# A two-layer graph network on one core: the gather loop, its tables and the order of the dense stages rewritten

## What is computed

```python
norm = -dinv[src] * dinv[dst]                       # dinv: 1/sqrt(degree)
def conv(x, W0, W1, b):
    tx1 = segment_sum(x[src] * norm[:, None], dst)  # gather rows, add them by target
    return x @ W0 + tx1 @ W1 + b
h = conv(x, W1_0, W1_1, b1)
h = layer_norm(h) * gamma + beta
h = where(h >= 0, h, 0.01 * h)
x = layernorm(x + conv(h, W2_0, W2_1, b2))
```

## Time and profile before

| | |
|---|---|
| runs without the profiler | 2444.04 us (2441.0 to 2445.28) |
| span of the profiled execution | 3370.7 us (the page gives no other time of it) |
| before the first gather | 201 us |
| layer 1, first to last gather | 201 to 1727 us |
| layer 2, first to last gather | 1775 to 3334 us |
| PE, DVE, ACT, POOL busy | 61%, 46%, 15%, 50% of the span |

### The profile page before, as it was taken

How to read it: one execution, slowest core, us unless ns; L and a number is a source line. 1 busy time by engine, 2 the same in 40 slices (tenths; PEclk the granted TensorE clock), 3 DMA queues, 4 the chain that set the end, 5 groups by cost and what they waited for, 6 DMA issues and landing times.

```text
span 3370.7 us, 41016 instructions
## 1 busy us (share of the span) xinstructions
PE 2065.1 (61%) x7250; PEld 963.6 (29%) x7251; DVE 1544.4 (46%) x3507; ACT 505.3 (15%) x1030; POOL 1700.9 (50%) x1725
## 2 busy tenths in 40 slices
PE   6836576665665665665764656565565656555655
PEld 5712232222222322232331222222222222222222
DVE  6754444444444444544443444444444434444444
ACT  5920111111111211111230000000000000000000
POOL 0156554545555554655526545554545445554543
PEclk6558887887887878887876878787777777878778
DMA  6376565655555555655646555565555555555554
GB/s 215 133 259 181 150 174 155 173 159 160 164 167 168 159 165 157 181 159 167 182 132 200 166 158 171 166 177 155 167 159 164 155 158 165 161 165 162 159 159 122
DMA packets 215109, 559.98 MB, mean 166 GB/s; under 512 B 48100, under 2 KB 49760, under 8 KB 214948
## 3 DMA queue, kind: packets, MB, share of 16 engines
q0 software_dynamic: 133120, 436.31, 45.9%
q10 hardware_dynamic: 44676, 81.73, 7.2%
q1 hardware_dynamic: 37152, 40.21, 3.6%
HBM read 493.08 MB, written 64.18 MB: 165 GB/s over the span
## 4 chain that ended last, share of the span: by engine, by line
PE 30%; another core or an unknown queue 26%; issue 25%; DVE 8%; ACT 5%; DVEq 3%; ACTq 1%; DMA 1%; POOL 1%; SPq 0%; POOLq 0%
PE bank L749 16%; PE bank L710 10%; DVE acc L947 6%; PE bank L668 2%; ACT work L556 2%; ACT feat L564 1%; DVEq L923 1%; PE bank L727 1%; PE bank L655 1%; DVEq L947 1%; DVE onehot L923 1%; POOL ring L444 1%; ACT work L546 1%; ACTq L528 0%
## 5 line engine op out<-in xcount | busy, mean ns | idle before, releaser
L444 POOL DMA_INDIRECT ring<-table,index x1664 | 1672.6, 1005 | 1466.5 <-SPq L393 952.1
L947 DVE SCALAR_TENSOR_TENSOR acc<-bank,down,acc 128x512 f32 x928 | 696.9, 751 | 1219.6 <-PE bank L710 709.8
L710 PE MATMUL bank<-ring,onehot 128*128 x3712 | 920.3, 406 | 306.0 <-issue 148.1
L749 PE MATMUL bank<-wA,feat 128*128 128x512 f32 x784 | 547.6, 863 | 804.2 <-ACT feat L564 748.2
L923 DVE TENSOR_SCALAR onehot<-count_h,dst_c,neg_tile 128x128 f16<-128x128 f16 x1856 | 489.2, 329 | 490.1 <-issue 487.6
L710 PEld LDWEIGHTS bank<-ring,onehot 128*128 128x128 f16 x3712 | 380.6, 103 | 865.6 <-issue 515.3
L749 PEld LDWEIGHTS bank<-wA,feat 128*128 128x128 f32 x784 | 212.0, 285 | 1084.9 <-ACT feat L564 774.3
L727 PE MATMUL bank<-wB,base_in 128*128 128x512 f32 x784 | 353.6, 594 | 0.0
L546 ACT ACTIVATE work<-acc 128x512 f32 (+1 forms) x98 | 61.7, 630 | 1747.4 <-issue 1039.3
L727 PEld LDWEIGHTS bank<-wB,base_in 128*128 128x128 f32 x784 | 149.5, 191 | 155.8 <-issue 142.1
L564 ACT ACTIVATE feat<-bank 128x512 f32<-128x512 f32 x98 | 58.5, 597 | 845.4 <-remote 828.7
(11 more groups left out here) (118 smaller groups left out, 689.6 us busy)
## 6 DMA issues: line engine op xcount, KB each, us to landing
ring<-table,index POOLq DMA_INDIRECT x1664
base_in<-feat ACTq DMA_DIRECT2D x98, 256.0 KB
feat<-feat SPq DMA_DIRECT2D x49, 256.0 KB, 2.9
table<-work SPq DMA_DIRECT2D x49, 256.0 KB, 3.1
feat<-feat ACTq DMA_DIRECT2D x49, 256.0 KB
table<-work ACTq DMA_DIRECT2D x49, 256.0 KB
feat<-in_x ACTq DMA_DIRECT2D x48, 256.0 KB
out<-work ACTq DMA_DIRECT2D x48, 256.0 KB
```

The source lines that it names most:

```text
L444: nc.gpsimd.indirect_dma_start(out=ring[:, at * ROW:(at + 1) * ROW], out_offset=None, in_=table[l], in_offset=bass.IndirectOffsetOnAxis(ap ...
L710: last = nc.tensor.matmul(bank[u % SUM_BANKS][:, :], onehot[:, u, j, :], ring[:, bass.ds(at, D)], start=j + half == 0, stop=j + half == GROUP)
L749: last = nc.tensor.matmul(to[:, :], feat[:, 2 + tile_slot, c * P:(c + 1) * P], wA[:, c * D:(c + 1) * D], start=False, stop=c == KB - 1)
L947: nc.vector.scalar_tensor_tensor(tile_of(acc, tile[u]), bank[u % SUM_BANKS][:, :], col(down[:, l, :], tile[u]), tile_of(acc, tile[u]), ALU ...
```

## The change

1. **Gathers.** The `bounds_check` register and `oob_is_err=False` are gone, and the indices are read straight from the columns of one table `index` for all 832 chunks; SP's copies L371 go. POOL's and SP's loops are written out in full.
2. **Register tables.** For each step one row of `step_u` (u16) holds the group and the four ring offsets, ready to be loaded; `tile_u` holds the offset of the tile in `acc`. PE and DVE are written out in full, four steps to a register load.
3. **One-hots.** `rel[:, n*2+j]` (fp16) holds, for each step's chunk, the targets relative to the step's tile. It is made ahead of the loop by 14 comparisons (`pick`) and 14 matmuls on PE. DVE then writes the one-hots of four steps (eight chunks) in one `tensor_tensor` of 128x1024 instead of eight `tensor_scalar` of 128x128.
4. **Adds.** The scale `down` is no longer applied in each step; a tile's sums are turned by a matmul with a scaled identity, `diag`, that ACT writes.
5. **Dense stages.** A visit now turns the sums of tile v and multiplies those of tile v-1 (moved by ACT since the visit before). The later stages lag 2 and 3 visits, not 3 to 6. Layer norm reads PSUM in layer 1. Visits come every 9.47 steps, at any step.
6. **Ahead of the first layer.** DVE makes the steps' tables after the first 8 of the 49 rows of L878 (L876 in the new file), not after all 49. The load of `wA` waits for `picked`.

```diff
@@ SP
-                def pass_on(it, l=l):
...
-                    if it.least + 2 < GATHER_BLOCKS:
-                        stage_index(it.n + 2, it.slot)
+                for g in range(GROUPS):
...
+                    sp.wait_ge(ring_landed[k], 16 * GROUP * ((GROUPS * l + g) // RING + 1))
+                    sp.sem_inc(groups_ready[l], 1)
@@ GpSimd
-            bound = pool.snap(pool.to_reg(N - 1))
...
-                            nc.gpsimd.indirect_dma_start(
-                                out=ring[:, at * ROW:(at + 1) * ROW], out_offset=None, in_=table[l],
-                                in_offset=bass.IndirectOffsetOnAxis(ap=index[:, it.slot, at:at + 1], axis=0),
-                                bounds_check=bound, oob_is_err=False).then_inc(ring_landed[k], 16)
+                        nc.gpsimd.indirect_dma_start(
+                            out=ring[:, at * ROW:(at + 1) * ROW], out_offset=None, in_=table[l],
+                            in_offset=bass.IndirectOffsetOnAxis(ap=index[:, c:c + 1], axis=0)
+                        ).then_inc(ring_landed[k], 16)
@@ VectorE
-                        last = nc.vector.tensor_scalar(onehot[:, slot, j, :], count_h[:, :],
-                                                       col(dst_c, group * GROUP + j), col(neg_tile, n),
-                                                       ALU.subtract, ALU.is_equal)
+                nc.vector.tensor_tensor(onehot[:, b % 2, :, :], count_h[:, :].unsqueeze(1).to_broadcast([P, HOTS, P]),
+                                        rel[:, b * HOTS:(b + 1) * HOTS].unsqueeze(2).to_broadcast([P, HOTS, P]),
+                                        ALU.is_equal).then_inc(onehots_ready, 1)
...
-                        nc.vector.scalar_tensor_tensor(tile_of(acc, tile[u]), bank[u % SUM_BANKS][:, :],
-                                                       col(down[:, l, :], tile[u]), tile_of(acc, tile[u]),
-                                                       ALU.mult, ALU.add).then_inc(sums_added, 1)
+                    nc.vector.tensor_tensor(acc_at, acc_at, bank[n % SUM_BANKS][:, :], ALU.add).then_inc(sums_added, 1)
@@ VectorE, ahead of the first layer
+            for b in range(EDGE_BLOCKS):
+                for j in range(GROUP):
+                    last = nc.vector.tensor_scalar(pick[b][:, :, j], group_f, (j - b * P) / GROUP, part_group[:, 0:1],
+                                                   ALU.add, ALU.is_equal)
@@ TensorE, in a visit
+                    dense(to, base_in[:, k.slot, :], wB, True)
...
+                    pe.wait_ge(sums_moved, TILES * l + k.n + 1)
+                    dense(to, sums_t[k.slot], wA, False).then_inc(out_done, 1)
+                if it.within(0, TILES):
...
+                    for c in range(KB):
+                        last = nc.tensor.matmul(bank[TURN_BANK][:, c * P:(c + 1) * P],
+                                                acc[:, bass.ds(it.n * D + c * P, P)], diag[:, it.slot, :],
+                                                start=True, stop=True)
+                    last.then_inc(sums_turned, 1)
```

More of the change, by code:

```diff
@@ L31 @@
 U32 = mybir.dt.uint32
+U16 = mybir.dt.uint16
 ALU = mybir.AluOpType
@@ new lines, in step @@
+            def step(l, n, entry):
+                g = STEPS * l + n
+                for j in range(GROUP):
+                    hot = onehot[:, n // BLOCK % 2, n % BLOCK * GROUP + j, :]
+                    for half in range(2):
+                        if j + half == 0:
+                            if n % BLOCK == 0:
+                                pe.wait_ge(onehots_ready, g // BLOCK + 1)
+                            if n == 0:
+                                wait(pe, sums_added, g - SUM_BANKS + 1)
+                            pe.wait_ge(groups_ready[l], entry[0])
+                        if j == GROUP - 1 and half == 1 and n + 1 < STEPS:
+                            wait(pe, sums_added, g + 1 - SUM_BANKS + 1)
+                        last = nc.tensor.matmul(bank[n % SUM_BANKS][:, :], hot,
+                                                ring[:, bass.ds(entry[1 + 2 * j + half], D)],
+                                                start=j + half == 0, stop=j + half == GROUP)
+                last.then_inc(steps_done[l], 1)
@@ new lines, in _ @@
+            for l in range(2):
+                for n in range(STEPS):
+                    if n % BLOCK == 0:
+                        entry = nc.values_load_multi_w_load_instructions(
+                            step_u[0:1, n * ENTRY:(n + BLOCK) * ENTRY], engines=[mybir.EngineType.PE], min_val=0,
+                            max_val=RING * GROUP * ROW - D, skip_runtime_bounds_check_because=WALK_FITS)[1]
+                    step(l, n, entry[n % BLOCK * ENTRY:(n % BLOCK + 1) * ENTRY])
+                    for v in range(TILES):
+                        if place(v) == n + 1:
+                            with pe.If(early > v):
+                                visit(numbered(v), n + 1, l)
+                visits_late(pe, early, (LAG_HIDDEN, LAG_SUMS)[l], lambda it, steps: visit(it, steps, l), True)
@@ L861, in _ @@
+            assert all(place(v) == FIRST_PLACE + (v * SPACING >> 8) for v in range(BOUNDS)) and place(BOUNDS) == STEPS
+            link(nc.vector.tensor_scalar(place_i[:, 0:1], part_i[:, :], SPACING, None, ALU.mult))
             link(nc.vector.tensor_scalar(place_i[:, 1:2], place_i[:, 0:1], 8, None, ALU.arith_shift_right))
             link(nc.vector.tensor_copy(place_f[:, 0:1], place_i[:, 1:2]))
-            link(nc.vector.tensor_tensor(place_f[:, 1:2], place_f[:, 0:1], part[:, :], ALU.add))
@@ L873, in _ @@
[L873 to L874 removed]
+            nc.vector.tensor_tensor(late[0:BOUNDS, 1:2], late[0:BOUNDS, 0:1], bound_f[0:BOUNDS, 2:3], ALU.mult
+                                    ).then_inc(walk_cmp, 1)
             def low_rows(it):
@@ L898, in _ @@
+            for b in range(2):
+                hots(0, b)
             dve.wait_ge(s_bias, 32)
```

728 lines of the change are left out of this document (372 added, 356 removed).

## The result

The changed kernel takes 2773.86 us (2768.18 to 2783.63, four runs) against 2444.18 us (2441.0 to 2445.28, four runs): ratio 1.136, 95% interval 1.133 to 1.1385. It is slower by 330 us, and 464 above my 2310. Its profiled execution has a span of 2766.3 us, like its runs.

What follows compares the result with a forecast made beforehand. The prediction took POOL's back-to-back gathers, 1.305 us apart, to bound the kernel. It summed 2444 - 225 (gathers) + 89 (one-hots) + 10 (start) - 9 (layer change) = 2309, said 2310 us; its own range 2230 to 2430, wider 2120 to 2545.

Steps and rivals of the forecast that it cites:

- What bounds the kernel before: POOL's gathers, one after the other: 1664 x 1.305 us plus 286.0 around them, 2457.5 against 2444.0 in runs.
- the 913 us of waits in the profiled execution: Other waits in POOL's gather loop, most traced to ACT's late L564; taken as mostly the profiled execution's own.
- PE needs 17.8 us in a tile: PE's 8.4 us of steps plus 9.4 of visit, against POOL's 22.2: 4.4 us to spare per tile.
- the visits, "only cover": Dense-stage visits: PE's shorter waits free time POOL's bound didn't need; 18.1 us of PE a tile, no gain counted.
- Gathers, 1.305 to 1.17: Removing the bounds check shortens the distance between POOL's gathers: 1664 x 0.135 = 225 us less, range 0 to 391.
- the check costs nothing: Rival: gather distance stays 1.305 us and the one-hots stall gathers by 80 us: 2525, slower; chance 0.34.
- One-hots, +89: DVE's two-input one-hot instruction, taken at 1.13 us, delays gathers starting beside it: 89 us more; 22 at 0.57 us.
- Adds 0: DVE's L947 adds without the scale save nothing, since DVE has 6 us to spare; PE's diag turn is hidden.
- start +10: DVE makes the tables after row 8, 13 us in which ACT stops: 10 us more until the first gather.
- layer change -9: Gap between layers, 48.2 us: the last visits' drain goes from 6 visits to 3, 9 us less.
- the unrolled program starves for instructions (nothing in the trace speaks for it): Rival on instruction supply, dismissed since PE's matmuls follow at 0.22 us with a register instruction between; no chance given.
- The prediction's last sign: POOL's waits for SP should be short; if long although its distance fell, PE or the transfers bind.

Runs made afterwards that it cites:

- p1: Kernel before without the gathers' bounds check, two register tables in 16 bits, undisturbed: 2362.0 us, ratio 0.966.
- h1: Kernel before with the second gather of each group left out from the ring's second turn, two tables in 16 bits, undisturbed: 2044.7 us, ratio 0.836.
- late sets: The three sets of experiments (first, second, fourth) beside which the kernel before took 3442 to 3453 us.
- n2: Changed kernel with PE loading 8 numbers per four steps, not 20, and the gathers' bounds check put back, undisturbed: 2545.0 us, ratio 1.043.
- m1: Changed kernel with PE loading 8 numbers (four 16-bit, four 32-bit) per four steps in place of 20, undisturbed: 2469.6 us, ratio 1.011.
- n1: Changed kernel with PE's 8-number loads and a block's one-hots written by eight tensor_scalar instructions, undisturbed: 2388.4 us, ratio 0.977.
- undisturbed: Condition of the four sets of experiments beside which the kernel before took 2442 to 2445 us.
- e1: Kernel before without the gathers' bounds check, two register tables in 16 bits, kernel before at 3448.7 us: 3443.7 us, ratio 0.9997.
- the first set: Four variants, one of the kernel before and three of the changed kernel, run where the kernel before took 3448.7 us.
- the sixth: Two variants of the changed kernel with small PE loads, scalar one-hots or the check put back, run where the kernel before took 2442.2 us.

## Why the prediction was wrong

**What bounds the kernel before: right.** The gathers did: p1, with shorter gathers and somewhat longer register loads, falls by 83 us where 1664 x (1.305 - 1.25) = 92 were to be had, and h1 falls to PE's side. That the 913 us of waits in the profiled execution weren't part of the runs of 2444 us was right too. Their origin was not: they aren't the profiler's, since the same kernel takes 3440 without it in the late sets. And "PE needs 17.8 us in a tile" was right within 1% (h1: 2044.7 for 2030).

**The step that failed: the visits, "only cover", with 18.1 us of PE a tile after the change.** I counted PE's matmuls and waits and none of the instructions of its sequencer. Part 2 of the change, the register tables, has no line in the prediction at all; under the gathers and the rivals I wrote that register work costs nothing, from rows where it was one instruction between gathers or matmuls. The change makes PE load 40 numbers in eight steps in place of 16, in 16 bits each, and the load of 4.73 us per four steps can't be hidden behind 3.6 us of matmuls, the less as it starts 2.0 us into them. PE's side went from 17.8 to 25 us a tile, above POOL's 21 to 22: +304 us. The numbers in reach before the run were two rows of the trace that I hadn't asked for (L698 above: 0.59 for eight numbers). They would have given 20 x 0.074 = 1.5 us, too little to show, by this estimate; in the traces it is the width of the number that makes 4.7 of it. A changed kernel with 20 numbers of 32 bits was not run.

The Trainium skill has the figure, in "Runtime: NRT & Kernel Launch", "Instruction fetch mechanics": about 200 ns for a register in a `TENSOR_LOAD`, also in bulk (the page speaks of the runtime's own loads, from HBM). For 16-bit numbers this case's traces agree (0.236 us each at 20, 0.238 at 14, 0.25 at 4), for 32-bit ones they don't (0.074 at 8, 0.083 at 4). By it an estimate of the load is 20 x 0.2 = 4.0 us, which is already above the block's 3.6 us of matmuls: it spoke against this change, and I didn't look for it. The floor of some 600 ns that the Trainium skill, in "DMA: Bandwidth & Descriptors", "Latency and other measured facts", gives for such a load isn't seen: four 32-bit numbers take 0.33.

**Gathers, 1.305 to 1.17: mis-sized.** The distance became 1.25 (0.95 + 0.30), worth 92 us and not 225; measured 83 (p1) and 75 (n2 against m1). The check is 0.055 of the 1.00 us, about an eighteenth, where I had guessed an eighth or a little more; no row had shown it. The rival "the check costs nothing", said to decide from 1.257 up, was nearer than my figure.

**One-hots, +89: right, once it can be seen.** The instruction took 1.218 us (1.13 taken), and without it the gathers-bound kernel gains 81 us (n1). In the changed kernel itself the gathers were 106 us longer than 1664 x 0.946, and PE's loads hid it. The Trainium skill reports in "SBUF — State Buffer", "Who interferes with whom", that `tensor_tensor` was not seen to stall DMAs that GpSimd issues; this case doesn't bear that out: the same one-hots as `tensor_scalar` leave the gathers at 0.953 in the mean, as `tensor_tensor` at 0.998.

**Adds 0, start +10, layer change -9.** First gather at 213.6 (201.3 before): +12. POOL's wait between the layers is 56.3 in the changed kernel and 48.5 in m1; in p1, the old order, undisturbed, it is 37.7 (48.2 in the profile of before). So the shorter lag doesn't shorten it: +11. The end of m1 is 36.3 behind the start of the last gather, of p1 26.4: +10, where the prediction had 0.

**The sum with the measured terms.** 2444 - 75 (check) + 81 (one-hots) + 12 + 11 + 10 = 2483 for m1, measured 2470; with the loads, +304, the changed kernel. What the 13 us between are is open; with p1's 83 for the check they are about 5. The forecast's other error, 225 for 92, would by itself have made it 2443 of 2310, so without the loads the change would have brought nothing (m1: 1.011).

Of the rivals, "the unrolled program starves for instructions (nothing in the trace speaks for it)" was nearest to what happened: PE did stand still for its own sequencer, though for a load of registers. I had dismissed it with a row of single register instructions. The prediction's last sign came true as well: POOL's waits for SP, 342 us in the changed kernel and 73 in m1, say that PE's side binds.

## What to carry to other kernels

Count the sequencer's work of a change as well as its engine's: a register load costs by the number, about 0.24 us for each 16-bit one and 0.07 to 0.08 for each 32-bit one on PE here, and it hides only behind the matmuls that have been issued already. The pauses that it makes can cost again behind them: here matmuls ran at half the clock after one of 5.3 us. Leave out of a table what an address can add as a constant.

When an engine's pauses have the same place and different releasers, ask for every instruction of its queue in that window, register instructions too, before moving other engines' work. And before trusting a profile to price a bound, take away the supposed bound (half of the gathers) once: it tells in one run which side sets the time. When a profile's span and the runs differ by more than a third, look for a second condition of the program before blaming the profiler.

## What was not expected of the hardware

**Two conditions of one program.** p1 and e1 are the same program, 2362.0 us in one set and 3443.7 in another. Chip number 15 showed both conditions, in the first set and in the sixth, so it is no fixed property of a chip. The line of DVE's adds and ACT's wait, first in p1, then in e1:

```profile
L949 DVEq FUSED_REGOPS  x928: 80/90/117, 214.2 to 2339.6; - x186
L949 DVE SCALAR_TENSOR_TENSOR acc<-bank,down,acc x928: 735/751/754, 214.3 to 2339.8; 128x512 f32 x186
ACT feat L565 <- PE bank L656: 159.2, 98, 3.4
```

```profile
L949 DVEq FUSED_REGOPS  x928: 13/93/708, 213.1 to 3412.0; - x186
L949 DVE SCALAR_TENSOR_TENSOR acc<-bank,down,acc x928: 737/751/753, 213.3 to 3412.2; 128x512 f32 x186
ACT feat L565 <- remote: 479.0, 80, 14.1
ACT feat L565 <- PE bank L656: 20.9, 16, 3.8
```

The adds (median 751 ns) and the gathers (947 and 946) are as long as ever; what changes is that a register instruction can take 0.7 us (of the short ones 710 take over 0.5 us in e1, 3 in p1) and that waits end by something that the profile hasn't recorded, here after up to 14.1 us. The wait of the earlier trace rows is one of these. The changed kernel has it less (2774 to 2959, where before goes from 2444 to 3450), so the sign of the comparison turns there: 1.136 undisturbed, 0.859 late. It is there with the bounds check and without (e1). What makes it, and why the written-out program suffers less, was not found; the old one has twice the short register instructions (18,700 and 9,000), but that this is the reason is a guess that no run tested.

**A register load's price is by number and by width.** 0.33 us for four 32-bit numbers, 0.59 for eight; 0.99 for four 16-bit ones on PE, 3.33 for 14, 4.73 for 20. Two tables show the width alone, eight numbers each: PE's groups take at least 0.59 us in 32 bits (before) and 1.92 in 16 (p1), SP's table `used` 0.53 in 32 bits (before) and 1.66 in 16 (after), in the median.
